# Graph layer and gated feed-forward on one core: where the first layer norm's reciprocal root is taken, bias matmuls of 512 columns, scatters in one run

## What is computed

```
n   = layernorm(x)                       # (x - mean) / sqrt(var + 1e-5)
agg = segment_sum(n[nbr], dst)           # over the edges
cnt = number of edges of each target
x   = x + n @ W1.T + b1 + (agg / max(cnt, 1)) @ W2.T + b2
n2  = layernorm(x)
x   = x + shared_mlp(n2) + sum of the two best of four expert MLPs, by a softmax gate
```

## Time and profile before

| | |
|---|---|
| median of 3 runs | 3190.23 us (3190.14 to 3193.08) |
| the profiled execution | 3193.37 us, its span 3191.8 us |
| first pass | from 0 to about 855 us |
| busy over the span | PE 97%, DVE 84%, ACT 61%, POOL 58% |
| mean granted TensorE clock | 0.988 |

### The profile page before, as it was taken

The page is one execution under the profiler, slowest core; times in us unless marked ns, Lnnn a source line. Parts: engine busy times, 40 slices in busy tenths (PEclk is TensorE's granted clock), DMA queues, the critical chain, the costliest instruction groups (busy, mean ns, idle before and its releaser), DMA issues.

```text
span 3191.8 us, 61476 instructions
## 1 busy us (share of the span) xinstructions
PE 3083.1 (97%) x20817; PEld 2822.4 (88%) x20817; DVE 2671.9 (84%) x7211; ACT 1942.1 (61%) x3507; POOL 1842.0 (58%) x1554
## 2 busy tenths in 40 slices
PE   7999899999689999999999999999999999999998
PEld 7999899999678888889898989888888888888887
DVE  8988898885288888888888888888888888888886
ACT  5655565556455656565656566666666666666665
POOL 1788888888665555555555555555555555555540
PEclk9999999999899999999999999999999999999999
DMA  7777677777533333333333333333333333333320
GB/s 242 212 219 207 192 211 202 197 202 210 148 100 100 86 99 87 98 88 95 92 93 92 92 91 92 93 89 97 86 99 85 100 85 101 85 101 85 98 79 27
DMA packets 201824, 387.38 MB, mean 121 GB/s; under 512 B 106671, under 2 KB 109821, under 8 KB 201506
## 3 DMA queue, kind: packets, MB, share of 16 engines
q1 hardware_dynamic: 133906, 226.02, 26.0%
q10 hardware_dynamic: 30800, 102.42, 10.0%
q0 software_dynamic: 36800, 54.95, 7.4%
HBM read 236.11 MB, written 161.00 MB: 124 GB/s over the span
## 4 chain that ended last, share of the span: by engine, by line
PE 71%; POOL 1%; issue 0%; DVE 0%; ACT 0%; DMA 0%; POOLq 0%; DVEq 0%
PE acc L1127 25%; PE acc L1188 13%; PE acc L1097 13%; PE acc L1108 4%; PE acc L1110 4%; PE acc L1174 3%; PE acc L1151 3%; PE acc L1184 2%; PE acc L1143 1%; PE acc L1199 1%; PE acc L1137 1%; POOL rows L165 0%; DMA rows<-z_d,tab 0%; POOL e_oh L177 0%; ACT h2f L1232 0%
## 5 line engine op out<-in xcount | busy, mean ns | idle before, releaser
L165 POOL DMA_INDIRECT rows<-z_d,tab x500 | 580.2, 1160 | 612.7 <-DMA tab<-tab_d 478.7
L177 POOL TENSOR_SCALAR e_oh<-iota_sb,tab 128x250 fp32r<-128x250 f32 (+1 forms) x500 | 522.2, 1055 | 460.8 <-PE acc L1110 452.3
L1127 PE MATMUL acc<-x1T_hi,wl_hl 128*128 128x500 f32 x2400 | 665.4, 392 | 0.0
L386 POOL DMA_INDIRECT tab_d<-pair,idx x400 | 550.5, 1376 | 118.6 <-issue 112.0
L725 PE MATMUL acc<-w_hl,xT_hi 128*125 128x256 f32 x3200 | 575.1, 285 | 0.1
L1127 PEld LDWEIGHTS acc<-x1T_hi,wl_hl 128*128 128x128 f32 x2400 | 444.0, 188 | 84.0
L1188 PE MATMUL acc<-wl_hl,h_hi 128*125 128x256 f32 x2400 | 479.1, 282 | 0.0
L725 PEld LDWEIGHTS acc<-w_hl,xT_hi 128*125 128x125 f32 x3200 | 470.6, 190 | 0.0
L1389 DVE TENSOR_TENSOR h_lo<-h1f,h_hi 128x500 fp32r<-128x500 f32 x600 | 397.3, 676 | 48.9 <-ACT h_hi L1226 40.5
L1219 ACT ACTIVATE h1f<-acc,bl_sb 128x500 f32<-128x500 f32 x600 | 404.3, 674 | 14.4
L1188 PEld LDWEIGHTS acc<-wl_hl,h_hi 128*125 128x125 f32 x2400 | 391.8, 186 | 3.7
(11 more groups left out here) (144 smaller groups left out, 6384.5 us busy)
## 6 DMA issues: line engine op xcount, KB each, us to landing
xs<-in_x SPq DMA_DIRECT2D x100, 448.0 KB
z_d<-zs ACTq DMA_DIRECT2D x100, 448.0 KB
y_d<-ys ACTq DMA_DIRECT2D x100, 448.0 KB
y_sb<-y_d SPq DMA_DIRECT2D x100, 448.0 KB
x_sb<-in_x SPq DMA_DIRECT2D x100, 448.0 KB
out<-x_sb SPq DMA_DIRECT2D x100, 448.0 KB
codes_b<-code_d SPq DMA_DIRECT2D x25, 390.6 KB
rows<-z_d,tab POOLq DMA_INDIRECT x500
```

What stands on the lines that cost most here:

```text
L165: pool.indirect_dma_start(out=rows[g.h][:, q, :], out_offset=None, in_=z_d, in_offset=bass.IndirectOffsetOnAxis(ap=tab[g.h][:, q, 0:1], ax ...
L177: pool.tensor_scalar(e_oh[:, q, w], iota_sb[:, w], tab[g.h][:, q, 1:2].bitcast(F32), None, ALU.is_equal).then_inc(S["e_oh_ready"], 1)
L386: pool.indirect_dma_start(out=tab_d, out_offset=bass.IndirectOffsetOnAxis(ap=idx[:, n:n + 1], axis=0), in_=pair[:, 2 * n:2 * n + ROW], in_ ...
L1127: mm = pe.matmul(bank[L1_BANKS[t]][:, 0:GN], wl1_hl[:, w, f, t * P:(t + 1) * P], (x1T_hi, x1T_lo)[a][:, f, :], start=n == 0, stop=n == 5)
```

## The change

- a_rstd is no longer made by GpSimd's power. ScalarE takes the root of a_var (`deviation`, a_std), VectorE the reciprocal of that (a_r0), and one Newton step r0 * (1.5 - 0.5 * var * r0 * r0) in three more operations, in `neg_bias` ahead of a_nb.
- On ScalarE deviation(0) stands first of all, deviation(1) between norm(0) and high(0), and deviation(g/2+2) in even g between the first and the second half of rows(g).
- The bias is held twice side by side; one matmul of 512 columns writes it for two parts, in place of two of 256. Two more small VectorE operations make the second copy at the start.
- GpSimd issues its 400 scatters in one loop, with no rstd between them and no group index. Their waits on s_idx, on the filled table and on the eighth scatter before stay.

```diff
--- before.py
+++ after.py
@@ -192,7 +192,7 @@
 
             with ExitStack() as c0:
                 w12_hl = sb("w12_hl", [P, 2, FT, 2 * D], F32R, c0)
-                bias_r = sb("bias_r", [P, D], F32R, c0)
+                bias_r = sb("bias_r", [P, 2, D], F32R, c0)
                 two_ones = sb("two_ones", [P, SP_], F32R, c0)
                 st_w12 = sb("st_w12", [P, FT, 2 * D], F32, c0)
                 st_wl1 = sb("st_wl1", [P, FT, H1T * P], F32, c0)
@@ -238,6 +238,10 @@
                 a_var = sb("a_var", [SP_, 8, NS], F32, c0)
                 a_rstd = sb("a_rstd", [SP_, 8, NS], F32, c0)
                 a_nb = sb("a_nb", [SP_, 8, NS], F32, c0)
+                a_std = sb("a_std", [SP_, 8, NS], F32, c0)
+                a_r0 = sb("a_r0", [SP_, 2, NS], F32, c0)
+                a_sq = sb("a_sq", [SP_, 2, NS], F32, c0)
+                a_cr = sb("a_cr", [SP_, 2, NS], F32, c0)
 
                 s_src = sem("sources_loaded")
                 s_dst = sem("targets_loaded")
@@ -275,6 +279,8 @@
                 a_stats = sem("a_stats_ready")
                 a_mean = sem("a_mean_ready")
                 a_varr = sem("a_var_ready")
+                a_sd = sem("a_std_ready")
+                a_nt = sem("a_newton_step")
                 a_rs = sem("a_rstd_ready")
                 a_nbr = sem("a_nb_ready")
                 a_xn = sem("a_xn_ready")
@@ -363,18 +369,6 @@
 
                     @block.gpsimd
                     def _(pool):
-                        pool.wait_ge(s_bs, 3)
-
-                        def rstd(m):
-
-                            u = 2 * m % 8
-                            pool.wait_ge(a_varr, m + 1)
-                            if m >= 4:
-                                pool.wait_ge(a_nbr, m - 3)
-                            pool.tensor_tensor(a_rstd[:, u:u + 2].rearrange("p g s -> p (g s)"),
-                                               a_var[:, u:u + 2].rearrange("p g s -> p (g s)"),
-                                               half_neg[0:SP_, :], ALU.pow).then_inc(a_rs, 1)
-
                         def scatter(n):
                             if n == 0:
                                 pool.wait_ge(s_filled, 16 * NFILL)
@@ -389,19 +383,8 @@
                                 in_=pair[:, 2 * n:2 * n + ROW], in_offset=None,
                                 bounds_check=NROW - 1, oob_is_err=False)\
                                 .then_inc(s_scat[n % NSC], 16)
-                        rstd(0)
-                        rstd(1)
-                        for g in range(NG):
-                            if g >= G_SCAT:
-                                n = min(EC, (g - G_SCAT) * 9 // 2)
-                                m = min(EC, (g + 1 - G_SCAT) * 9 // 2)
-                                for e in range(n, min(n + 3, m)):
-                                    scatter(e)
-                            if g % 2 == 0 and g + 4 < NG:
-                                rstd(g // 2 + 2)
-                            if g >= G_SCAT:
-                                for e in range(n + 3, m):
-                                    scatter(e)
+                        for e in range(EC):
+                            scatter(e)
                         for h in range(NSC):
                             pool.wait_ge(s_scat[h], 16 * (EC // NSC))
                         pool.nop().then_inc(s_alltab, 1)
@@ -438,15 +421,28 @@
                                        .then_inc(a_mean, 1)
                             dve.wait_ge(a_mean, 2 * NS * (m + 1))
                             if m >= 4:
-                                dve.wait_ge(a_rs, m - 3)
+                                dve.wait_ge(a_nt, 3 * (m - 3))
                             dve.tensor_scalar(a_var[:, u:u + 2], a_mv[:, u:u + 2, :, 1], EPS, None,
                                               ALU.add).then_inc(a_varr, 1)
 
                         def neg_bias(m):
                             u = 2 * m % 8
-                            dve.wait_ge(a_rs, m + 1)
+                            dve.wait_ge(a_sd, m + 1)
                             if m >= 4:
                                 dve.wait_ge(a_xn, 2 * NS * (m - 3))
+                            dve.reciprocal(a_r0[:], a_std[:, u:u + 2]).then_inc(a_nt, 1)
+                            dve.wait_ge(a_nt, 3 * m + 1)
+                            dve.tensor_tensor(a_sq[:], a_r0[:], a_r0[:], ALU.mult)\
+                               .then_inc(a_nt, 1)
+                            dve.wait_ge(a_nt, 3 * m + 2)
+                            dve.scalar_tensor_tensor(out=a_cr[:], in0=a_sq[:], scalar=-0.5,
+                                                     in1=a_var[:, u:u + 2], op0=ALU.mult,
+                                                     op1=ALU.mult).then_inc(a_nt, 1)
+                            dve.wait_ge(a_nt, 3 * m + 3)
+                            dve.scalar_tensor_tensor(out=a_rstd[:, u:u + 2], in0=a_cr[:], scalar=1.5,
+                                                     in1=a_r0[:], op0=ALU.add,
+                                                     op1=ALU.mult).then_inc(a_rs, 1)
+                            dve.wait_ge(a_rs, m + 1)
                             dve.scalar_tensor_tensor(out=a_nb[:, u:u + 2], in0=a_mv[:, u:u + 2, :, 0],
                                                      scalar=-1.0, in1=a_rstd[:, u:u + 2],
                                                      op0=ALU.mult, op1=ALU.mult).then_inc(a_nbr, 1)
@@ -582,9 +578,10 @@
                         dve.wait_ge(s_bs, 4)
                         dve.tensor_copy(st_bh[:], st_bs[:]).then_inc(s_bs, 1)
                         dve.wait_ge(s_bs, 5)
-                        dve.tensor_tensor(bias_r[32:33], st_bs[:], st_bh[:].bitcast(F32),
-                                          ALU.subtract).then_inc(s_bs, 1)
-                        dve.tensor_copy(bias_r[0:1], st_bh[:].bitcast(F32)).then_inc(s_bs, 1)
+                        for k in range(2):
+                            dve.tensor_tensor(bias_r[32:33, k], st_bs[:], st_bh[:].bitcast(F32),
+                                              ALU.subtract).then_inc(s_bs, 1)
+                            dve.tensor_copy(bias_r[0:1, k], st_bh[:].bitcast(F32)).then_inc(s_bs, 1)
                         dve.wait_ge(s_whi, 1)
                         dve.tensor_tensor(w12_hl[:, 1], st_w12[:], w12_hl[:, 0].bitcast(F32),
                                           ALU.subtract).then_inc(s_wlo, 1)
@@ -632,6 +629,14 @@
 
                     @block.scalar
                     def _(act):
+                        def deviation(m):
+                            u = 2 * m % 8
+                            act.wait_ge(a_varr, m + 1)
+                            if m >= 4:
+                                act.wait_ge(a_nt, 3 * (m - 4) + 1)
+                            act.activation(a_std[:, u:u + 2], a_var[:, u:u + 2],
+                                           ACT.Sqrt).then_inc(a_sd, 1)
+
                         def norm(g):
                             act.wait_ge(a_nbr, g // 2 + 1)
                             if g:
@@ -662,9 +667,11 @@
                             hl, st = ((wl1_hl, st_wl1), (wl2_hl, st_wl2), (wl3_hl, st_wl3))[n]
                             act.copy(hl[:, 0], st[:]).then_inc(s_fhi, 1)
 
+                        deviation(0)
                         act.wait_ge(s_w12, 16 * 3)
                         act.copy(w12_hl[:, 0], st_w12[:]).then_inc(s_whi, 1)
                         norm(0)
+                        deviation(1)
                         high(0)
                         norm(1)
                         for a, to in ((2, gbase), (3, second)):
@@ -687,6 +694,8 @@
                                 norm(g + 2)
                             half_rows(g, 0, zs, 4, s_z, a_z)
                             half_rows(g, 0, ys, 2, s_y, a_y)
+                            if g % 2 == 0 and g + 4 < NG:
+                                deviation(g // 2 + 2)
                             if G_WTS <= g < G_WTS + 3:
                                 high_weights(g - G_WTS)
                             half_rows(g, 1, zs, 4, s_z, a_z)
@@ -717,14 +726,17 @@
                             cols_ = slice(s * SP_, (s + 1) * SP_)
                             for b, wt in ((2, slice(0, D)), (4, slice(D, 2 * D))):
                                 o = bank[b + s // 2][0:SP_, (s % 2) * D:(s % 2 + 1) * D]
-                                if b == 2:
-                                    pe.matmul(o, two_ones[:], bias_r[:], start=True, stop=False)
+                                if b == 2 and s % 2 == 0:
+                                    pe.matmul(bank[b + s // 2][0:SP_, :], two_ones[:],
+                                              bias_r[:].rearrange("p k d -> p (k d)"),
+                                              start=True, stop=False)
                                 n = 0
                                 for a, w in PARTS:
                                     for f in range(FT):
```

(5 more changed lines are left out.)

## The result

The changed kernel takes 3211.4 us (median of 5 runs, 3206.6 to 3212.2) against 3192.4 us before: ratio 1.006, interval 1.0048 to 1.0071. It is slower by 0.6%. The forecast was 3187 us in a range of 3156 to 3208.

What follows compares the result with a forecast made beforehand. GpSimd was taken to bound the first pass, and a new VectorE-ScalarE ring to pace it afterwards. Terms -15.1 + 3.9 + 3.0 + 3.7 + 1.3 = -3.2 us from 3190.2 gave 3187 us, 8-in-10 range 3156 to 3208.

Steps and rivals of the forecast that it cites:

- rival 4: First pass: GpSimd was not the bound, so the new work only costs; about 3200 us, chance 4%.
- The root's wait closes a ring that paces the pass: First pass, even groups: ScalarE waits for VectorE's variance, VectorE then for ScalarE's high half; 8.33 us per group against 34.2 per four.
- The size of the ring: First pass, low half through variance, root, second half, store and high half to the next low half: 8.47 us.
- 0.17 + 0.04: Ring term: us for VectorE's variance operation and its signal to ScalarE.
- I take 3.07: Ring term: us on ScalarE for second half of the rows and store, until the high half; the row read was 2.97.
- Groups 81 to 95: First pass after the chunks end: the ring stays at 15.40 us per pair, 107.8 against 103.9, 3.9 us more.
- The start: Before the first rows: the second root waits for the variance ahead of the first high half, 3.7 us more.
- Newton step 0.88 us: VectorE, odd groups: four small operations of 0.22 us per pair, 50 times; bounds 0.7 to 1.8 us.
- Table of functions: ScalarE, second pass or its start: one more table load for the exponential, 0 to 1.3 us, taken as 1.3.
- Rival 2: Ring longer than counted through ScalarE's store issues: some 60 at 0.4 us more, 24 us, 3211 us; chance 20%.
- Rival 1: Ring does not bind; the pass falls to the larger of VectorE (7.88 us per group) and PE (7.76): 3146 us, chance 18%.
- Rival 3: ScalarE changes the root's table in every pair, two loads of 1.283 us in 48 pairs: 123 us, 3310 us; chance 3%.

Runs made afterwards that it cites:

- e6: Kernel before with 8 scatters per two groups instead of 9, the 32 left over behind the loop: 3188.7 us; groups 9 to 81 took 560.4 us.
- e1: Changed kernel with ScalarE's root inside the loop taken one turn later, right behind the high half: 3158.2 us.
- e4: Changed kernel with one more unused ScalarE copy of 125x512 behind each root of the loop: 3226.9 us.
- e3: Kernel before, power still on GpSimd, with only ScalarE's wait for the variance added in even turns: 3200.3 us.
- e10: Changed kernel with its 400 scatters held back until the last slots are ready: 3666.2 us, only the pass is read; groups 9 to 81 took 599.5 us.
- e8: Changed kernel with two more tiny unused VectorE operations between variance and next comparison in even turns: 3210.5 us.
- e5: Changed kernel without the Newton step, the scale being the plain reciprocal of the root: 3191.7 us.
- e2: e1 with the second root at the start also moved, behind the norm of group 1: 3155.6 us.

## Why the prediction was wrong, point by point

- **GpSimd bounds the pass before: right.** e6 shows it, and with it that rival 4 is out.
- **The root's wait closes a ring that paces the pass: right.** e1 opens it (-53 us), e4 lengthens it (+15.5), e3 makes it without the root (+8). The pattern in the four turns was forecast as 8.47, 6.93, 8.54, 9.38 and is 8.89, 7.25, 8.83, 9.47.
- **The size of the ring: the step that failed.** In the part on the root, "0.17 + 0.04" for the variance and "I take 3.07" for the second half and the store. By turn, they and what stands beside them measured:
  - The 0.17 was read in a turn with the slots. In turn 0 it is mostly 0.46: 18 x 0.29 = 5.2 us. It was there to be read before: grouped over 100 to 700 us, the trace of the kernel before has 0.352 us in the mean for the same operation:

```profile
L442 DVE TENSOR_SCALAR a_var<-a_mv 125x8 f32<-125x8 f32 x35 | 12.3, 352 | 1.2
```

  - The 3.07 was one quiet row, 2.97, and a tenth. The mean of all turns from 100 to 700 us had already been 3.20 before; in turn 0 on the ring it is 3.23, in turn 1, which ScalarE's own queue paces, 3.40: 18 x (0.16 + 0.33) = 8.8 us.
  - In turn 2 the ring and VectorE were nearly equal (8.47 and 8.54), and the larger of two typical values was taken. Measured is 8.83, 0.29 above: 5.2 us. The ring itself had a mean of 8.67 there (variance 0.08 and store 0.12 longer than summed); the other 0.16 are turns in which the high half was ready and VectorE was not.
  - In turn 3, VectorE's own, 9.47 for 9.38: 1.6 us.

  Together 20.8, where 20.1 were missed. In e10, with GpSimd silent, the miss is gone: the variance is back at 0.17 us in every even turn, second half and store at 3.08 in turn 0 and 3.13 in turn 1. Why the latter are shorter there is open.
- **Groups 81 to 95: +3.9 forecast, +9.2 measured.** The sign was right, one item was left out of the sum: in turns 84 to 86 ScalarE also takes the high halves of three weight tensors between root and second half. They take 1.46, 0.85 and 0.82 us, and these three turns together were 2.5 us longer than the forecast's values. Turns 90 to 92 were 3.0 longer, with 4.13, 3.53 and 4.30 us for second half and store in place of 3.07, and a variance of 0.43 us in turn 92, which ended with an operation of GpSimd for the second pass. This is read from one trace and not tried; in e8 the stretch took 110.1.
- **The start: right,** 3.7 and 3.65. The root began at 22.50 where 22.3 was summed.
- **Newton step 0.88 us:** right, the four operations took 0.83 (402.65 to 403.48). That nothing but the chunk-heavy turns would pay for it was a little too kind (e5).
- **Earlier table worth nothing: right.** GpSimd's last scatter began at 771 us (765 forecast). But for 5 us at 818 (five operations on the first table) it then stood idle until z landed, in GpSimd's timeline:

```profile
876.31 1.14 POOL L165 DMA_INDIRECT rows<-z_d,tab  x1 [53.14 <-DMA z_d<-zs]
```

- **Table of functions: there, and hidden.** The 1.3 us in the sum are not seen in the time (the end took no longer, above). In ScalarE's timeline the second load stands ahead of the first exponential, which then waited for VectorE all the same:

```profile
914.96 1.28 ACT L1258 ACT_TABLE_LOAD   x1
916.97 0.22 ACT L1258 ACTIVATE ga<-z 125x16 f32<-125x16 f32 x1 [0.73 <-DVE z L1308]
```

- **Rival 2** (a longer ring; slower from some 0.2 us a store) is the one that came true. That its number, 3211, is the measured one is luck: it put 0.4 us on each of 60 stores, 24 us, and nothing elsewhere; the stores carried about 9 us in turns 0 and 1, the variance, turn 2 and the weights most of the rest. **Rival 1** was wrong for this order and nearly right for e1's and e2's: 8.0 us a group where it had 7.88, 3156 to 3158 us where it had 3146. **Rival 3** did not happen: two table loads in all.

With the root where e1 or e2 has it, the same change makes 3158.2 or 3155.6 us, 1.1% faster than before.

## What to carry to other kernels

When a step moves to another engine, its price can be less the instruction than the wait in front of it: here an added wait without any work cost 8 us (e3), and the same work behind the high half instead gave 53 (e1). Write down what is queued behind that wait, follow it round until it meets the engine that is waited for, and compare the length of this ring with each engine's own work. Sum the ring from means over many turns, not from one clean row, and where two bounds are within a few per cent of each other expect the real pace above both (turn 2: 8.83 for 8.67 and 8.54). If the operand is ready anyway a little later in the queue, put the step there.

## What the runs showed of the hardware

A scatter on GpSimd holds up small tensor_scalar operations of VectorE that begin in its later part until it ends. In the changed kernel, variances that began 0.63 to 0.84 us into a scatter of 1.19 us took 0.34 to 0.55 us, otherwise mostly 0.17; with GpSimd silent (e10) their mean is 0.172 for 0.359. The 16-bit comparisons fell from 0.417 to 0.346. With all that goes with it, silencing GpSimd gave 20 us of the pass (619.8 to 599.5 us for 72 groups). The scatters themselves were 1.366 us long in the mean in the changed kernel and 1.196 in e10, where they ran behind VectorE's work on the chunks; whether VectorE holds them up in turn was not tried.

Why the stores' issues on ScalarE are also shorter with GpSimd silent (3.13 for 3.40 us in turn 1, with the two copies of the second half ahead of them) is not settled: e10 takes the scatters' memory traffic out of the pass together with GpSimd's work.
